# A sliding-window attention stage: new issue orders, probabilities scaled on VectorE, and first loads sorted by use

## The chip, the cores and the metric

The kernel runs on one core of a Trainium2 chip. The metric is the device time of one execution in microseconds (us), lower is better. Four engines compute: TensorE (PE in the profile: matmuls and transposes, results go to PSUM), VectorE (DVE), ScalarE (ACT) and GpSimd (POOL). SyncE (SP) issues most DMAs. Every engine runs its own instruction stream in order, and they wait for one another by semaphores.

## The reference, cut to what matters

Four residual blocks on x of shape (8, 512, 256), float32, one after the other: attention with relative position tables, a mixture of experts, sliding-window attention, the same mixture again. Before each block comes a layernorm. The third block is the one whose instruction orders change:

```
q = rmsnorm(x @ wq.T) * q_gamma ; k = rmsnorm(x @ wk.T) * k_gamma ; v = x @ wv.T      # 16 heads of 64
scores = q @ k.T / 8 + slope[head] * (j - i);  masked unless 0 <= i - j <= 128
attn = softmax(scores);  out = attn @ v;  x = x + out @ wo.T
```

## The kernel before

There are six stages, each with a program per engine: `relative_stage` (tag a), the mixture (`shared_stage` and `expert_stage`, tags fs and fe), `window_stage` (tag b), and the mixture again (gs and ge). Stages don't overlap, except by a few instructions.

`window_stage` works in tiles of 128 queries, 4 to a batch element and 32 in all. With a window of 128, a tile sees its own 128 keys and the 128 before them; the first tile of a batch element has only its own (`lo = 1`). It is called the short tile here, the other three full tiles. For a tile, TensorE does 4 `scores` steps of 4 heads, 8 `probs_T` steps (transposes of the probabilities of 2 heads) and 8 `values` steps. Between them lie the sections of a neighbouring tile: `x` (transposes of the normed input), `q`, `k`, `v` (2 halves each, 6 matmuls of 512 columns a half), `q_T`, `k_T` (2 halves each), `out` (24 matmuls), `xn_T`, and after the last tile of a batch element `gate`. All sections write the one PSUM bank `ps_w`, so each waits until the section before it is copied out (`bank_free`): by VectorE for q, k, q_T, out and gate, by ScalarE for v, k_T and xn_T, by both in turn for x.

The softmax of two heads (index k from 0 to 7) goes: `biased` on VectorE adds the bias and takes the minimum of the negated scores (L1433), `exp` on ScalarE writes `prob` and the row sums (L1315), `inverse` on VectorE takes reciprocals (L1438), `divide` on GpSimd multiplies `prob` of both heads by them (L1377), `probs_T` on TensorE transposes (L1264), VectorE copies that to SBUF (L1442), and `values` multiplies by v (L1275).

What each engine does in which order within a tile is written out in the lists WINDOW_ORDER (TensorE), WINDOW_SCALAR_ORDER, WINDOW_VECTOR_ORDER, WINDOW_POOL_ORDER and WINDOW_SYNC_ORDER. An entry is (step, index, offset in tiles): ("q", 0, 1) is the first half of q for the next tile. `rounds` runs the lists: two partial rounds before the first tile, batch elements 0 and 1 unrolled, 2 to 6 in a hardware loop over the batch element (4 back-edges), 7 unrolled, two rounds behind. In the partial round (-1, 3), the step before the first tile, `first` calls `split_weights`, which casts the weights (ScalarE: high part, VectorE: rest), before that round's own steps.

Besides the divides, GpSimd has the powers (`x_pow`, `pow`, `y_pow`) and `normed`, two instructions of 128x1024 each tile (L1372).

In `relative_stage`, 13 constant tables are loaded after x, all counted by one semaphore `const_in`. TensorE (L1986, then 64 small matmuls L1995 that fold table ends into weights), ScalarE and VectorE wait for all 13. VectorE's set-up (L2376 to L2424) is one long chain, whose last part needs the folded products in `ps_w`; only then does TensorE begin the first q (L2008).

## Time and profile before

| | |
|---|---|
| median of 3 runs | 3860.88 us (3854.68 to 3863.89) |
| the profiled execution's own time | 3863.76 us |
| its span, first to last instruction | 3861.9 us |
| TensorE busy over the span | 3522.0 us (91%) |
| VectorE / ScalarE / GpSimd busy | 2448.2 (63%) / 1814.1 (47%) / 1055.7 (27%) us |
| window stage, 2060 to 3045 us: TensorE / VectorE / ScalarE / GpSimd busy | 915.0 / 623.9 / 482.8 / 363.8 us |

A row of the timeline gives the start and the length in us, the engine, the line, the tiles written and read, the form and the count, and in brackets how long the engine had been idle and what released it. An engine's next instruction can start a little before the listed end of the last, so steps are counted from start to start. PEclk is the share of TensorE's full clock of 2.4 GHz that was granted; 0.5 is 1.2 GHz. Idle time counts only on the engine that everybody waits for.

### The profile page before, as it was taken

The numbers are of one execution on the slowest core, as the hardware profiler recorded it, in microseconds if no ns is written. First come the engines' busy times: TensorE is split into PE (matmuls) and PEld (weight loads), VectorE is DVE, ScalarE is ACT, GpSimd is POOL, SyncE is SP. The second block draws the span as 40 slices with busy tenths as digits, with TensorE's granted clock in tenths as the row PEclk, the third lists the DMA queues.
The fourth block names the chain that finished last, engine by engine and source line by source line (L and its number), as shares of the span: only waits on it lengthen the run. The fifth ranks groups of instructions, "written<-read, shape, count | busy, mean of one in ns | idle before, by whom it ended". The sixth has DMA issues, their size and how long they took to land. (4 is left out here: it accounts for less than half of the span.)

```text
span 3861.9 us, 92551 instructions
## 1 busy us (share of the span) xinstructions
PE 3522.0 (91%) x33008; PEld 2702.7 (70%) x33008; DVE 2448.2 (63%) x5451; ACT 1814.1 (47%) x3734; POOL 1055.7 (27%) x1031
## 2 busy tenths in 40 slices
PE   5999999999997968999995999999999795999998
PEld 3666666666665857888884777667767684888887
DVE  3676666666665666666753666666666576676664
ACT  1665665665663323444442555445545332444443
POOL 0222222222221002333421433334333101243332
PEclk9999999999998989999996999999999897999999
DMA  4565565565564223434422000000000123343441
GB/s 149 162 172 165 155 176 163 159 177 167 155 176 123 89 93 112 131 102 116 120 65 79 16 21 21 19 19 21 21 19 16 60 87 112 110 120 110 118 117 31
DMA packets 349199, 390.10 MB, mean 101 GB/s; under 512 B 155377, under 2 KB 292721, under 8 KB 335345
## 3 DMA queue, kind: packets, MB, share of 16 engines
q1 hardware_dynamic: 324210, 351.18, 29.3%
q0 software_dynamic: 24576, 33.57, 5.0%
q8 instruction: 240, 3.93, 0.4%
q14 instruction: 173, 1.42, 0.1%
HBM read 246.97 MB, written 137.69 MB: 100 GB/s over the span
## 5 line engine op out<-in xcount | busy, mean ns | idle before, releaser
L2278 POOL TENSOR_TENSOR a_below<-a_probT,a_upper 128x512 f32<-128x512 f32 x128 | 164.2, 1283 | 743.8 <-DVE a_probT L2476 553.4
L2213 ACT ACTIVATE a_prob<-a_ps_s,a_low 128x512 f32<-128x512 f32 x512 | 318.3, 692 | 53.1 <-DVE a_low L2496 52.7
L1377 POOL TENSOR_TENSOR b_prob<-b_prob,b_rinv 128x512 f32<-128x512 f32 (+1 forms) x256 | 237.8, 934 | 383.1 <-DVE b_rinv L1438 383.0
L2060 PE MATMUL a_ps_p<-a_ident,a_prob 128*128 128x128 f32 x2048 | 315.8, 288 | 12.9 <-ACT a_band L2190 9.0
L2496 DVE TENSOR_REDUCE a_low<-a_ps_s 128x2 f32<-128x1024 f32 x256 | 313.5, 1225 | 8.8
L1315 ACT ACTIVATE b_prob<-b_score,b_low 128x256 f32<-128x256 f32 (+1 forms) x512 | 241.8, 474 | 125.4 <-DVE b_low L1433 114.4
L2060 PEld LDWEIGHTS a_ps_p<-a_ident,a_prob 128*128 128x128 f32 x2048 | 222.1, 143 | 101.2 <-issue 75.8
L2186 ACT COPY a_probT<-a_ps_p 128x512 f32<-128x512 f32 x352 | 195.1, 590 | 171.6 <-PE a_ps_p L2060 171.0
L1433 DVE CUSTOM_DVE_ANT_0 b_score<-b_ps_s,b_bias 128x256 f32<-128x256 f32 (+1 forms) x512 | 178.1, 386 | 74.3 <-PE b_ps_s L1256 72.1
L2495 DVE TENSOR_TENSOR a_ps_s<-a_ps_s,a_win 128x320 f32<-128x320 f32 (+1 forms) x256 | 135.0, 527 | 133.5 <-PE a_ps_s L2093 131.0
L611 POOL DMA_INDIRECT out<-ge_eo,ge_index_scatter x64 | 120.7, 1886 | 361.4 <-DVE ge_eo L806 346.7
L611 POOL DMA_INDIRECT x<-fe_eo,fe_index_scatter x64 | 120.6, 1884 | 361.6 <-DVE fe_eo L806 347.0
L198 ACT ACTIVATE fe_gelu<-fe_ps_g 128x512 f32<-128x512 f32 x128 | 76.5, 598 | 287.6 <-PE fe_ps_u L177 287.6
L198 ACT ACTIVATE ge_gelu<-ge_ps_g 128x512 f32<-128x512 f32 x128 | 76.5, 598 | 287.5 <-PE ge_ps_u L177 287.5
L1442 DVE COPY b_probT<-b_ps_p 128x512 f32<-128x512 f32 (+1 forms) x256 | 155.5, 617 | 60.8 <-PE b_ps_p L1264 59.3
L214 DVE TENSOR_TENSOR fe_raw<-fe_gelu,fe_ps_u 128x512 f32<-128x512 f32 x128 | 88.0, 687 | 158.0 <-ACT fe_gelu L198 147.0
L214 DVE TENSOR_TENSOR ge_raw<-ge_gelu,ge_ps_u 128x512 f32<-128x512 f32 x128 | 88.0, 687 | 157.8 <-ACT ge_gelu L198 146.8
L1275 PE MATMUL b_ps_o<-b_probT,b_v 128*64 128x128 f32 x1792 | 149.5, 287 | 4.7 <-DVE b_probT L1442 3.8
L187 PE MATMUL fe_ps_d<-fe_d_rest,fe_h_high 128*128 128x256 f32 x512 | 144.3, 282 | 9.8 <-DVE fe_eo L806 6.9
L187 PE MATMUL ge_ps_d<-ge_d_rest,ge_h_high 128*128 128x256 f32 x512 | 144.3, 282 | 9.8 <-DVE ge_eo L806 6.9
L1264 PE MATMUL b_ps_p<-b_ident,b_prob 128*128 128x128 f32 x896 | 147.1, 281 | 4.4 <-POOL b_prob L1377 4.4
L2476 DVE COPY a_probT<-a_ps_p 128x512 f32<-128x512 f32 x160 | 110.4, 691 | 63.2 <-PE a_ps_p L2060 61.4
(437 smaller groups left out, 10433.6 us busy)
## 6 DMA issues: line engine op xcount, KB each, us to landing
a_win<-band SPq DMA_DIRECT2D x128, 384.0 KB, 5.3
prob<-a_prob SPq DMA_DIRECT2D x128, 384.0 KB, 3.7
shift<-a_gbias SPq DMA_DIRECT2D x64, 256.0 KB, 2.0
a_shifted<-shift SPq DMA_DIRECT2D x256, 64.0 KB, 2.1
a_bins<-prob SPq DMA_DIRECT2D x128, 128.0 KB, 3.7
fe_gT<-in_WgT SPq DMA_DIRECT2D x16, 1024.0 KB
fe_uT<-in_WuT SPq DMA_DIRECT2D x16, 1024.0 KB
fe_dT<-in_WdT SPq DMA_DIRECT2D x16, 1024.0 KB, 4.9
```

The costliest lines, as they stand in the source:

```text
L187: last = nc.tensor.matmul(ps_d[t // 2][:, t % 2, :], h[b][:, slot, t * P:(t + 1) * P], d[a][:, j, :], start=(j == 0 and t % 2 == 0 and (a, ...
L214: nc.vector.tensor_tensor(raw[:, slot % 2, :], gelu[:, slot % 2, :], ps_u[slot % 2][:, :], ALU.mult).then_inc(h_ready, 1)
L611: nc.gpsimd.indirect_dma_start(rows_y, bass.IndirectOffsetOnAxis(index[1][:, q, t:t + 1], 0), eo[:, q, t, :], None, bounds_check=B * T - 1 ...
L1315: nc.scalar.activation(prob[:, h % 8, lo * P:], score[:, h % 8, lo * P:], ACT.Exp, bias=low[:, h % 8:h % 8 + 1], scale=-1.0, accum_out=rsu ...
L1377: nc.gpsimd.tensor_tensor(part, part, by_row, ALU.mult).then_inc(divided, 1)
L1433: nc.vector.tensor_tensor_reduce(out=score[:, h % 8, lo * P:], in0=ps_s[k // 2 % 2][r][:, k % 2, lo * P:], in1=bias[:, h, lo * P:], scale= ...
L1442: nc.vector.tensor_copy(probT[:, k % 2, :, lo:, :], ps_p[k % 2][:, :, lo:, :]).then_inc(copied, 1)
L2060: last = nc.tensor.transpose(bank[:, c * P:(c + 1) * P], prob[:, t % 2, h, 32 + c * P:32 + (c + 1) * P], ident[:, :])
L2186: last = nc.scalar.copy(probT[:, t % 2, h, :], ps_p[i][:, :])
L2213: nc.scalar.activation(prob[:, t % 2, h, 32:32 + T], ps_s[pair][:, r, :], ACT.Exp, bias=low[:, h:h + 1]).then_inc(exped, 1)
L2278: nc.gpsimd.tensor_tensor(below[:, t % 2, :, :], probT[:, t % 2, :, t * P:(t + 1) * P], upper[:, :].unsqueeze(1).to_broadcast([P, HG, P]), ...
L2496: nc.vector.reduce_max(low[:, 2 * pair:2 * pair + 2], both[:, :, :], AX.X, negate=True).then_inc(maxed, 1)
```

## The change

Three things are changed together:

1. All five order lists of the window stage are written anew. On TensorE, `v` 1 moves from the tile's end to its middle, `gate` stands directly behind `q_T` 0, and `k_T` 1 ends the tile. On VectorE, `probs_T` 6 and 7 are done at the end of their own tile and no longer at the start of the next; `x_normed` stands first. The load of x is issued two tiles ahead, not three.
2. `divide` moves from GpSimd to VectorE and takes in `inverse`: a reciprocal, a wait for it, and then one `tensor_scalar` for each of the two heads (128x256, in a short tile 128x128) in place of one broadcast `tensor_tensor` over both.
3. Set-up. In `relative_stage` the loads are split over three semaphores: first ident, table, rows, base (`const_in`), then seven small ones (`small_in`), then the two weights (`w_in`); TensorE and VectorE wait for each only where it is used, ScalarE for none. In `window_stage`, ScalarE's `split_weights` and VectorE's `set_gains` now come before all rounds. The first tile's `x_normed` is an entry of round (-1, 3), and so comes behind VectorE's `split_weights`; before it was an entry of the round ahead of that.

```diff
 WINDOW_ORDER = [
     ("scores", 0, 0), ("x", 0, 1), ("scores", 1, 0), ("out", 0, -1), ("probs_T", 0, 0), ("q", 0, 1), ("scores", 2, 0), ("q", 1, 1),
-    ("probs_T", 1, 0), ("values", 0, 0), ("k", 0, 1), ("scores", 3, 0), ("k", 1, 1), ("probs_T", 2, 0), ("values", 1, 0), ("xn_T", 0, -1),
-    ("probs_T", 3, 0), ("v", 0, 1), ("values", 2, 0), ("gate", 0, -1), ("probs_T", 4, 0), ("q_T", 0, 1), ("values", 3, 0), ("probs_T", 5, 0),
-    ("q_T", 1, 1), ("probs_T", 6, 0), ("values", 4, 0), ("k_T", 0, 1), ("values", 5, 0), ("probs_T", 7, 0), ("k_T", 1, 1), ("values", 6, 0),
-    ("values", 7, 0), ("v", 1, 1),
+    ("scores", 3, 0), ("k", 0, 1), ("values", 0, 0), ("probs_T", 1, 0), ("k", 1, 1), ("probs_T", 2, 0), ("values", 1, 0), ("v", 0, 1),
+    ("probs_T", 3, 0), ("values", 2, 0), ("xn_T", 0, -1), ("values", 3, 0), ("v", 1, 1), ("probs_T", 4, 0), ("probs_T", 5, 0), ("q_T", 0, 1),
+    ("gate", 0, -1), ("probs_T", 6, 0), ("values", 4, 0), ("q_T", 1, 1), ("values", 5, 0), ("probs_T", 7, 0), ("k_T", 0, 1), ("values", 6, 0),
+    ("values", 7, 0), ("k_T", 1, 1),
 ]
 WINDOW_SCALAR_ORDER = [
-    ("exp", 0, 0), ("exp", 1, 0), ("exp", 2, 0), ("exp", 3, 0), ("exp", 4, 0), ("q", 0, 1), ("q", 1, 1), ("k", 0, 1), ("exp", 5, 0), ("k", 1, 1),
-    ("xn_T", 0, -1), ("exp", 6, 0), ("v", 0, 1), ("exp", 7, 0), ("high", 0, 0), ("gate_exp", 0, -1), ("k_T", 0, 1), ("k_T", 1, 1), ("high", 1, 0),
-    ("v", 1, 1), ("x", 0, 2),
+    ("exp", 0, 0), ("exp", 1, 0), ("exp", 2, 0), ("exp", 3, 0), ("gate_exp", 0, -2), ("q", 0, 1), ("exp", 4, 0), ("q", 1, 1), ("k", 0, 1),
+    ("k", 1, 1), ("exp", 5, 0), ("v", 0, 1), ("xn_T", 0, -1), ("exp", 6, 0), ("high", 0, 0), ("v", 1, 1), ("exp", 7, 0), ("k_T", 0, 1),
+    ("high", 1, 0), ("k_T", 1, 1), ("x", 0, 2),
 ]
 WINDOW_VECTOR_ORDER = [
-    ("probs_T", 6, -1), ("probs_T", 7, -1), ("rest", 1, -1), ("biased", 0, 0), ("x", 0, 1), ("biased", 1, 0), ("inverse", 0, 0), ("biased", 2, 0),
...
+    ("x_normed", 0, 1), ("rest", 1, -1), ("biased", 0, 0), ("x", 0, 1), ("biased", 1, 0), ("biased", 2, 0), ("divide", 0, 0), ("biased", 3, 0),
+    ("out", 0, -1), ("divide", 1, 0), ("y_stats", 0, -1), ("q", 0, 1), ("divide", 2, 0), ("y_mean", 0, -1), ("biased", 4, 0), ("q", 1, 1),
+    ("probs_T", 0, 0), ("divide", 3, 0), ("x_stats", 0, 2), ("k", 0, 1), ("biased", 5, 0), ("probs_T", 1, 0), ("y_var", 0, -1), ("biased", 6, 0),
+    ("k", 1, 1), ("x_mean", 0, 2), ("gate_end", 0, -2), ("probs_T", 2, 0), ("y_normed", 0, -1), ("mean", 0, 1), ("biased", 7, 0),
+    ("probs_T", 3, 0), ("x_var", 0, 2), ("divide", 4, 0), ("divide", 5, 0), ("divide", 6, 0), ("probs_T", 4, 0), ("rest", 0, 0), ("q_T", 0, 1),
+    ("probs_T", 5, 0), ("gate", 0, -1), ("divide", 7, 0), ("q_T", 1, 1), ("probs_T", 6, 0), ("probs_T", 7, 0),
 ]
 WINDOW_POOL_ORDER = [
-    ("divide", 0, 0), ("divide", 1, 0), ("divide", 2, 0), ("x_pow", 0, 2), ("y_pow", 0, -1), ("divide", 3, 0), ("divide", 4, 0), ("pow", 0, 1),
-    ("normed", 0, 1), ("divide", 5, 0), ("divide", 6, 0), ("normed", 1, 1), ("divide", 7, 0),
+    ("y_pow", 0, -1), ("pow", 0, 1), ("normed", 0, 1), ("x_pow", 0, 2), ("normed", 1, 1),
 ]
 WINDOW_SYNC_ORDER = [
-    ("store", 0, -1), ("store_turned", 0, -2), ("store_normed", 0, -1), ("load", 0, 3),
+    ("store_normed", 0, -2), ("load", 0, 2), ("store", 0, -1), ("store_turned", 0, -1),
 ]
...
+                    elif kind == "divide":
+                        dve.wait_ge(exped, 16 * w + 2 * k + 2)
+                        nc.vector.reciprocal(rinv[:, p, 2 * k:2 * k + 2], rsum[:, p, 2 * k:2 * k + 2]).then_inc(rinv_ready, 1)
+                        dve.wait_ge(rinv_ready, 8 * w + k + 1)
+                        for r in range(2):
+                            h = 2 * k + r
+                            part = prob[:, h % 8, lo * P:]
+                            scaled = nc.vector.tensor_scalar(part, part, rinv[:, p, h:h + 1], None, ALU.mult)
+                        scaled.then_inc(divided, 1)
...
-                    set_gains()
                     split_weights()
                 unit(b, t)
 
+            set_gains()
             rounds(nc.vector, first)
...
+        first_loads = ((ident, const["ident"]), (whole_table, table_d), (rows, rows_d), (whole_base, base_d))
+        small_loads = ((upper, const["upper"]), (iota, const["iota"]), (number, const["token"]), (scale, const["row_scale"]),
+                       (bins_w, bins_d), (bins_b, bins_base_d), (vbase, vbase_d))
+        w_loads = ((wT, wT_d[0]), (wv, wT_d[1]))
```

## Rows read from the trace of the kernel before

**Rows 1.** Busy time of each engine by stretch: one query tile each, PEclk the granted clock
```profile
2220.41:2249.10 28.69, 26.03 (x178) 18.59 (x177) 16.02 (x69) 13.41 (x49) 8.81 (x13) 1.00 0.06 20
2249.10:2277.43 28.33, 28.23 (x210) 20.93 (x209) 20.46 (x70) 15.18 (x48) 12.21 (x13) 1.00 0.06 19
2421.38:2453.60 32.22, 28.74 (x210) 20.96 (x209) 19.97 (x67) 15.81 (x49) 12.22 (x13) 1.00 0.06 19
2453.60:2484.91 31.31, 28.76 (x177) 21.00 (x177) 16.41 (x69) 13.02 (x48) 8.85 (x13) 0.89 0.06 19
```

**Rows 2.** Timeline in a short tile: start, length, engine, line
```profile
2227.84 0.69 DVE L1414 COPY b_raw<-b_ps_w 128x512 f32<-128x512 f32 x1 [0.30 <-PE b_ps_w L1191]
...
2228.59 0.50 PE L1191 MATMUL b_ps_w<-b_wq_high,b_x_rest 128*128 128x512 f32 x1
```

**Rows 3.** Timeline near the end of a full tile
```profile
2272.44 1.28 DVE L1442 COPY b_probT<-b_ps_p 128x512 f32<-128x512 f32 x2
...
2273.79 0.66 PE L1264 MATMUL b_ps_p<-b_ident,b_prob 128*128 128x128 f32 x4
...
2274.28 0.60 PE L1198 MATMUL b_ps_w<-b_ident,b_normed 128*128 128x128 f32 x4
...
2274.81 1.09 PE L1275 MATMUL b_ps_o<-b_probT,b_v 128*64 128x128 f32 x16
```

**Rows 4.** Timeline of the first stage's start
```profile
16.13 0.17 DVE L2376 MEMSET a_v<- 128x128 f32 x1 [0.17 <-DVE a_prob L2374]
...
21.24 2.40 DVE L2380 TENSOR_TENSOR a_win<-a_probT,a_win 128x1040 f32<-128x1040 f32 x2 [4.95 <-DMA a_scale<-in_row_scale]
...
23.02 13.65 PE L1995 MATMUL a_ps_w<-a_probT,a_k_up 128*128 128x4 f32 x64
...
35.05 0.24 DVE L2415 TENSOR_SCALAR a_query_same<-a_iota,a_residue 128x32 f32<-128x32 f32 x1
36.71 0.51 DVE L2420 COPY a_k_low<-a_ps_w 128x32 f32<-128x32 f32 x4 [1.43 <-PE a_ps_w L1995]
...
41.14 0.79 PE L2008 MATMUL a_ps_w<-a_x_high,a_w_rest 128*128 128x512 f32 x1 [4.47 <-DVEq L2431]
```

**Rows 5.** DMA issues of the first 60 us: count, KB, us from issue to landing
```profile
a_win<-in_a_base SPq DMA_DIRECT2D x1, 1040.0 KB, 11.5
```

**Rows 6.** Timeline of the window stage's start
```profile
2074.25 2.18 ACT L1342 CAST b_wo_high<-b_prob 128x512 fp32r<-128x512 f32 x4 [0.24 <-DMA b_prob<-in_b_woT]
...
2078.49 0.77 PE L1191 MATMUL b_ps_w<-b_wq_high,b_x_rest 128*128 128x512 f32 x1 [11.12 <-DVE b_x_rest L161]
```

**Rows 7.** Groups of instructions by line and form, GpSimd and VectorE: busy us, mean ns
```profile
L1372 POOL TENSOR_SCALAR b_normed<-b_raw,b_rrms 128x1024 f32<-128x1024 f32 x64 | 71.6, 1119 | 15.3 <-POOL b_rrms L1366 14.1 <-DVE b_rinv L1438 1.2
...
L1363 POOL TENSOR_TENSOR b_rstd<-b_var,b_minus_half 128x1 f32<-128x1 f32 x32 | 17.5, 548 | 31.3 <-DVE b_var L1399 31.3
...
L1438 DVE RECIPROCAL b_rinv<-b_rsum 128x2 f32<-128x2 f32 x256 | 37.7, 155 | 12.1 <-ACT b_prob L1315 11.0 <-issue 0.9
...
L2340 DVE TENSOR_SCALAR a_xi<-a_xi,a_in_mv,a_in_rstd 128x256 f32<-128x256 f32 x32 | 11.3, 415 | 1.4 <-POOL a_in_rstd L2297 1.4
...
L842 DVE TENSOR_SCALAR fe_eo<-f_st,f_thr 128x512 f32<-128x512 f32 x1 | 0.5, 487 | 0.0
...
L2415 DVE TENSOR_SCALAR a_query_same<-a_iota,a_residue 128x32 f32<-128x32 f32 x1 | 0.2, 236 | 0.0
```

**Rows 8.** Timeline: VectorE and GpSimd at the same time
```profile
2204.17 1.04 POOL L1377 TENSOR_TENSOR b_prob<-b_prob,b_rinv 128x512 f32<-128x512 f32 x1 [0.22 <-DVE b_rinv L1438]
...
2204.58 0.78 DVE L1403 TENSOR_SCALAR b_xn<-b_x,b_mv,b_rstd 128x256 f32<-128x256 f32 x1
```

**Rows 9.** Timelines of VectorE and TensorE around a loop back-edge
```profile
2447.75 1.29 DVE L1442 COPY b_probT<-b_ps_p 128x512 f32<-128x512 f32 x2 [2.08 <-PE b_ps_p L1264]
...
2448.49 1.26 PE L1275 MATMUL b_ps_o<-b_probT,b_v 128*64 128x128 f32 x16 [1.06 <-DVE b_probT L1442]
...
2453.60 0.71 PE L1256 MATMUL b_ps_s<-b_kT,b_qT 64*128 64x128 f32 x8 [2.27 <-issue]
```

More of the change, by code:

```diff
@@ L912 @@
+    ("high", 1, 0), ("k_T", 1, 1), ("x", 0, 2),
 ]
 WINDOW_VECTOR_ORDER = [
-    ("probs_T", 6, -1), ("probs_T", 7, -1), ("rest", 1, -1), ("biased", 0, 0), ("x", 0, 1), ("biased", 1, 0), ("inverse", 0, 0), ("biased", 2, 0),
-    ("gate_end", 0, -2), ("biased", 3, 0), ("inverse", 1, 0), ("out", 0, -1), ("y_stats", 0, -1), ("probs_T", 0, 0), ("x_stats", 0, 2),
-    ("inverse", 2, 0), ("x_mean", 0, 2), ("q", 0, 1), ("y_mean", 0, -1), ("x_var", 0, 2), ("biased", 4, 0), ("q", 1, 1), ("y_var", 0, -1),
@@ L917 @@
-    ("probs_T", 1, 0), ("inverse", 3, 0), ("biased", 5, 0), ("x_normed", 0, 2), ("inverse", 4, 0), ("k", 0, 1), ("y_normed", 0, -1), ("k", 1, 1),
-    ("probs_T", 2, 0), ("biased", 6, 0), ("mean", 0, 1), ("probs_T", 3, 0), ("biased", 7, 0), ("inverse", 5, 0), ("gate", 0, -1),
-    ("inverse", 6, 0), ("probs_T", 4, 0), ("q_T", 0, 1), ("inverse", 7, 0), ("rest", 0, 0), ("q_T", 1, 1), ("probs_T", 5, 0),
+    ("x_normed", 0, 1), ("rest", 1, -1), ("biased", 0, 0), ("x", 0, 1), ("biased", 1, 0), ("biased", 2, 0), ("divide", 0, 0), ("biased", 3, 0),
@@ L1342, in split_weights @@
                     nc.scalar.copy(wo[0][:, i:i + 2, :].rearrange("p k c -> p (k c)"), flat[:, i * C:(i + 2) * C]).then_inc(wo_high, 1)
-            def first(b, t):
-                if isinstance(b, int) and (b, t) == (-1, NT - 1):
-                    split_weights()
-                unit(b, t)
-            rounds(nc.scalar, first)
+            split_weights()
+            rounds(nc.scalar, unit)
         @block.gpsimd
@@ L1372, in unit @@
                         nc.gpsimd.tensor_scalar(normed[:, k, :], raw[:, k, :], rrms[:, k:k + 1], 1.0, ALU.mult, ALU.mult).then_inc(normed_ready, 1)
-                    elif kind == "divide":
-                        reach_alone(pool, rinv_ready, 8 * w + k + 1)
-                        part = prob[:, 2 * (k % 4):2 * (k % 4) + 2, lo * P:]
-                        by_row = rinv[:, p, 2 * k:2 * k + 2].unsqueeze(2).to_broadcast([P, 2, (2 - lo) * P])
-                        nc.gpsimd.tensor_tensor(part, part, by_row, ALU.mult).then_inc(divided, 1)
                     elif kind == "y_pow":
@@ L1769, in relative_stage @@
         o_taken = s.sem("o_taken")
-        loads = ((ident, const["ident"]), (upper, const["upper"]), (iota, const["iota"]), (number, const["token"]), (wT, wT_d[0]), (wv, wT_d[1]),
-                 (rows, rows_d), (whole_table, table_d), (whole_base, base_d), (bins_w, bins_d), (bins_b, bins_base_d), (vbase, vbase_d),
-                 (scale, const["row_scale"]))
-        assert len(loads) == LOADS
+        first_loads = ((ident, const["ident"]), (whole_table, table_d), (rows, rows_d), (whole_base, base_d))
+        small_loads = ((upper, const["upper"]), (iota, const["iota"]), (number, const["token"]), (scale, const["row_scale"]),
+                       (bins_w, bins_d), (bins_b, bins_base_d), (vbase, vbase_d))
+        w_loads = ((wT, wT_d[0]), (wv, wT_d[1]))
+        assert len(first_loads + small_loads + w_loads) == LOADS
         block = ctx.enter_context(s.programs())
@@ L1824, in _ @@
             sp.dma_start(xi[:, :, :], by_token(x_d, 0)).then_inc(xi_in, 16)
-            for tile, dram in loads:
-                sp.dma_start(tile[tuple(slice(None) for _ in tile.shape)], dram).then_inc(const_in, 16)
+            for loads, sem in ((first_loads, const_in), (small_loads, small_in), (w_loads, w_in)):
+                for tile, dram in loads:
+                    sp.dma_start(tile[tuple(slice(None) for _ in tile.shape)], dram).then_inc(sem, 16)
             for sem in (x1_out, yn_out, ynT_out):
@@ L2151, in _ @@
         def _(act):
-            act.wait_ge(const_in, 16 * len(loads))
             def empty(kind, b, g, k=0):
```

9 lines of the change are left out of this document (7 added, 2 removed).

## Prediction

> **What bounds the kernel now.** I read the page's busy shares first, then the busy time of single query tiles in the window stage, then the timelines of the three places that the change touches: the start of the first stage, the start of the window stage, and its tiles.
>
> TensorE is busy for 91% of the span, but in the window stage that share hides two limits. A full tile takes 28.33 us with TensorE busy for 28.23 of them [rows 1]: TensorE never waits for anybody there, and no order can make the tile shorter (its neighbour took 28.37; I use 28.35). A short tile has fewer matmuls and still takes 28.69 us, with TensorE busy for 26.03 [rows 1]. What holds it is the one bank `ps_w`: after a section its result is copied out, and the next section starts only then. The copy of q starts at 2227.84 and takes 0.69 us, and TensorE's next section starts 0.75 us after the copy began [rows 2]. I added up the short tile section by section: x 1.4 us, out 3.6, six halves of q, k and v at 2.3 to 2.5, four of q_T and k_T at 1.3 to 1.6, xn_T 1.0, gate 2.5, each from its own start to the start of the next, gives 28.5 us, nearly all of the 28.69. So the short tile can't get much shorter either by an order; it only gets longer when a copy comes late.
>
> VectorE does most of these copies in order with everything else. It is busy for 20.46 us of the full tile and 16.02 of the short one [rows 1]: it has room, but not much.
>
> The tiles at a loop back-edge are longer: 32.22 us for the last one of an iteration and 31.31 us for the short one behind it, the latter at a mean granted clock of 0.89 [rows 1]. In the first of them TensorE waits 1.06 us for a copy of probabilities and then 2.27 us for nothing that the profile shows, its own branch [rows 9]. The copy was late since VectorE had its own back-edge just ahead of `probs_T` 6, and began only at 2447.75 after 2.08 us idle [rows 9]. There are 4 such places.
>
> **The change, part by part.** *Start of the first stage.* VectorE's last memset ends at 16.13 + 0.17 = 16.30 us; then it waits for all 13 tables until 21.24 [rows 4]. TensorE waits as long. From there VectorE's chain runs to 35.05 + 0.24 = 35.29, 14.05 us; the folding on TensorE ends at 23.02 + 13.65 = 36.67 [rows 4], 15.43 us after 21.24. VectorE goes on at 36.71 and the first q starts at 41.14 [rows 4]. Now only x, ident, table, rows and base are ahead: 3.6 MB instead of the 5.0 MB that were ahead of and with base when it landed at 5.38 + 11.5 = 16.9 us [rows 5]. In proportion they land at 13 to 14.5. VectorE then starts at 16.30 and is through at 30.35, TensorE at 14.5 + 15.43 = 29.9. So 36.71 becomes 30.4 to 30.6: 6.1 us gained. Bounds: if base still lands at 16.9, TensorE is through at 32.3, and 4.4 are left; if the small loads land no sooner than the last table did, at 21.24, VectorE has about 11.4 us left from there, and 4.1 are left. The two weights come last, 5.9 MB in all as before, so by 21 us, long before 30. Everything behind moves up by the same amount. Value -6.1, bounds -4.1 to -6.3.
>
> *Start of the window stage.* ScalarE's casts no longer wait for the first x_high, but the last four need wo, which landed at 2074.25 [rows 6], and the DMA order is the same. So VectorE ends its rests at most 0.4 us sooner (it was through at 2078.05). But the first tile's `x_normed` now stands behind them, and with it the transposes, ScalarE's cast and VectorE's rest of x: 0.42 + 0.69 + 0.37 + 0.42 and some 0.15 of waits, 2.05 us, where only the rest of 0.42 was left. The first q, at 2078.49 [rows 6], comes 1.3 us later; bounds 0.9 (if VectorE is through earlier still) to 1.7.
>
> *The divide itself.* It leaves GpSimd, where one took 1.04 us [rows 8], off the path but for its latency. On VectorE no such instruction is in the trace at this size, so its price comes from neighbours of the same kind. A `tensor_scalar` with one per-row scalar takes 487 ns for 512 columns and 236 for 32 [rows 7]: 0.52 ns a column, so 353 ns for 256 and 286 for 128. The next instruction starts about 0.08 us before the listed end (two copies of 0.68 end to end take 1.28 [rows 3]), so each costs 0.27 (0.21) us of the queue. With a reciprocal of 155 ns [rows 7] and the wait for it, 0.19, a divide is 0.73 us in a full tile and 0.61 in a short one; `inverse`, 0.08 of queue, goes. The upper bound is the nearest row with 256 columns and two such scalars, 415 ns [rows 7]: 0.33 each, 0.85 a divide. Eight divides add 5.2 us to VectorE's 20.46 less 0.7 for `x_normed` and `y_normed`, which now seldom meet GpSimd: 25 us of 28.3.
>
> By the Trainium skill (VectorE: DVE Perf Modes, section on the TRN2 errata) a float32 SBUF op that runs two elements a cycle costs 58 + 128 cycles at 256 columns, 0.19 us. No row has this; by it a full tile's late stretch below would be 0.6 us shorter, and the stall that I find there gone.
>
> *Full tile.* I laid VectorE's new list against TensorE's with these prices. Up to `probs_T` 3 VectorE catches up several times, so the eight copies and divides there are hidden. The tight stretch is behind it. TensorE's work after `probs_T` 3: six `values` at 0.59 (a pair together 1.03), four transposes of probabilities at 0.49, four of q and k at 0.53 [rows 3], v at 1.6, xn_T at 0.27: 9.4 us, so `probs_T` 3 is done at 28.35 - 9.4 = 18.95 of the tile. VectorE then has eight copies of 0.60 [rows 3], four divides of 0.73 and `x_var`, 7.8 us without a pause, to 26.8; after that TensorE has values 7 and k_T 1, 1.05 us. That fits inside 28.35 with 0.4 to spare.
>
> But GpSimd's `normed` is in the same stretch. It isn't free of VectorE: `x_normed` on VectorE, 415 ns elsewhere [rows 7], took 0.78 us when it started in the middle of a GpSimd instruction, and ended 0.15 us behind that one's end, 2204.17 + 1.04 against 2204.58 + 0.78 [rows 8]. In the new lists `x_pow` waits for `x_var`, just ahead of divides 4 to 6, takes 548 ns, and `normed` of 1119 ns [rows 7] follows at once: it starts about 0.9 us behind `x_var`, in the middle of divide 5. Whoever comes first, one of VectorE's four instructions there ends behind `normed`: 0.9 to 1.0 us later. The copies behind it move with it, 26.8 becomes 27.75, and the tile ends at 27.75 + 0.1 + 1.05 = 28.9: 0.55 us longer. The queue behind holds the copies that TensorE waits for (`q_T`, `probs_T` 5 to 7), so nothing hides it. I take 0.45 for 24 tiles, 10.8 us; bounds 0 (no collision, or spare time enough) to 1.0 (415 ns instead of 353 makes the eight late instructions 0.5 longer).
>
> The Trainium skill (SBUF — State Buffer, "Who interferes with whom") says that a VectorE instruction in a two-port mode and a GpSimd instruction exclude each other for their whole length. The row on `x_normed` agrees; without that rule the 10.8 us would be 0.
>
> *Short tile.* The same sections give the same sum, 28.5; the move of `gate` behind `q_T` 0 changes what fills the waits, not their number. The collision delays the copy of q_T 0 by 0.5, and TensorE waits for it directly: 0.2 longer than now after the 0.3 that better fillers give. 8 tiles, 1.6 us; bounds -2.4 to 5.
>
> *Back-edges.* VectorE's branch now lies behind `probs_T` 7, beside TensorE's own, so the 1.06 us goes, 4 times: -4.2. The 2.27 stays. Less idle time there may spare one or the other fall of the clock: -1, bounds -6 to +4. The exit of the stage has the same chain as before: 0, plus or minus 1.
>
> *Sum.* -6.1 + 1.3 + 10.8 + 1.6 - 4.2 - 1 = +2.4 us. The profiled execution took 3863.76 us itself, so 3866.2 by its measure; it lay 2.9 above the median of 3860.88, so 3863.3, rounded to 3863.
>
> **Rivals.** *A, nothing collides or VectorE has more room than I think:* full tiles stay at 28.35, short ones gain 0.3. -6.1 + 1.3 - 2.4 - 4.2 - 1 = -12.4, 3848. For it: 0.4 us spare in my own count, and the start of `normed` depends on 0.2 us either way. Against: `x_pow` and `normed` are tied to the same `x_var` as the divides.
>
> *B, VectorE becomes the bound:* the price is 415 ns and the collision full. Full tiles +1.0, short ones +0.6: -6.1 + 1.3 + 24 + 4.8 - 4.2 - 1 = +18.8, 3880. It decides from about 26.9 us of VectorE work in a full tile, or 0.4 us of delay behind `probs_T` 3. For it: eight late instructions in a row, each wait uncounted. Against: TensorE's stalls give VectorE time back at the start of the next tile.
>
> *C, the loads don't come sooner:* if DMA works the new order as late as the old one, set-up gains only 2 us or nothing and the rest stands: +6 to +8.5, 3867 to 3869. Against: transfers of the first 20 us are steady, and the order of issue is the order of landing.
>
> **How the numbers follow.** My forecast has 0.45 (own range 3854 to 3872), A 0.20, B 0.23, C 0.07, and 0.05 is left for what I don't see. 3863 is the forecast's. The range goes from A's to B's middle, 3847 to 3882; outside lie about 2 in 10. 0.2% is 7.7 us, what a measurement can just tell from no change. Faster (under 3853.2): A and a little of the forecast's, 0.23. Slower (over 3868.6): B, a fifth of the forecast's, half of C and the rest, 0.36. Same: 0.41.
>
> **What would show it.** In the first stage: VectorE's `tensor_tensor` L2380 near 16.4 us and the first q near 35. In the window stage: first q 1.3 us later against the stage's first load; `tensor_scalar` on prob near 353 ns in the median, but a part of 0.9 or more, those that end 0.15 us behind a `normed`; full tiles of 28.7 to 28.9 us, with TensorE's waits for q_T, k_T's turn and the last probabilities; no wait of 1.06 us ahead of the back-edge. I am wrong if full tiles stay at 28.35 (A), if they pass 29.2 (B), or if the first q of the kernel stays at 41 us (C).

## The result: 0.35% slower

| | before | after |
|---|---|---|
| median of 8 runs each, on the same chip | 3854.05 us (3843.55 to 3863.89) | 3869.89 us (3861.73 to 3874.4) |
| after / before | | 1.0035, 95% interval 1.002 to 1.005 |
| profiled execution, its span | 3863.76, 3861.9 us | 3865.24, 3863.5 us |

By the ratio that is +13.5 us (7.7 to 19.3). The forecast was 3863 with a range of 3847 to 3882: the range held the time, but the likeliest case said "no change that can be told", and it is a small loss. The forecast as a change was +2.4 us, added to a median of before of 3860.88; over eight runs that median is 3854.05, so the two times lie closer together (3863 and 3869.89) than the two changes do (+2.4 and +13.5). The two profiled executions are only 1.6 us apart. The profile of before was taken in an execution 9.7 us above that kernel's median here, that of after in one 4.7 us below its own, so the spans can't be compared, only the stages.

**Starts of the stages after.** The first group is the first stage (the rows to hold against [rows 4]), the second the window stage ([rows 6]).

```profile
14.24 13.65 PE L1998 MATMUL a_ps_w<-a_probT,a_k_up 128*128 128x4 f32 x64
...
16.07 2.37 DVE L2382 TENSOR_TENSOR a_win<-a_probT,a_win 128x1040 f32<-128x1040 f32 x2
...
34.45 0.77 PE L2012 MATMUL a_ps_w<-a_x_high,a_w_rest 128*128 128x512 f32 x1 [6.55 <-DVEq L2435]
```

```profile
2058.77 2.18 ACT L1341 CAST b_wo_high<-b_prob 128x512 fp32r<-128x512 f32 x4 [0.67 <-DMA b_prob<-in_b_woT]
...
2061.83 0.41 DVE L1393 TENSOR_SCALAR b_xn<-b_x,b_mv,b_rstd 128x256 f32<-128x256 f32 x1
...
2063.95 0.76 PE L1190 MATMUL b_ps_w<-b_wq_high,b_x_rest 128*128 128x512 f32 x1 [0.97 <-DVE b_x_rest L161]
```

The first q starts at 34.45 us, 6.7 us sooner. The window stage's first q comes 5.18 us behind the cast of wo; before it was 2078.49 - 2074.25 = 4.24. Measured from the end of TensorE's last product of the mixture ahead, it is 34.68 us against 33.69: 1.0 later.

**Tiles after.** Busy time by stretch, one tile each, columns as in [rows 1]: an unrolled short tile, the full tile behind it, the next one; then, in the loop, the tile that holds the back-edge, the short one behind it, and a second tile of a batch element.

```profile
2202.86:2231.46 28.60, 26.15 (x177) 18.57 (x176) 20.57 (x86) 13.48 (x49) 4.02 (x5) 1.00 0.06 20
2231.46:2260.65 29.19, 28.68 (x209) 20.89 (x209) 25.37 (x86) 15.25 (x49) 4.14 (x5) 1.00 0.06 19
2260.65:2289.28 28.63, 28.49 (x210) 20.89 (x209) 24.40 (x83) 15.22 (x49) 4.17 (x5) 1.00 0.07 20
2405.73:2437.57 31.84, 28.63 (x210) 20.93 (x209) 25.34 (x84) 15.98 (x50) 4.14 (x5) 0.99 0.06 19
2437.57:2471.66 34.09, 31.59 (x176) 23.15 (x177) 20.56 (x85) 12.85 (x47) 4.02 (x5) 0.80 0.06 18
2347.24:2376.84 29.60, 28.82 (x209) 20.93 (x208) 25.52 (x86) 15.29 (x49) 4.14 (x5) 1.00 0.06 20
```

"Second tile" is from here on the one behind the short tile, and a plain full tile is the third or fourth outside the loop. Plain full tiles went from 28.35 to 28.63 us, second tiles from 28.33 to 29.19 (in the loop 28.59 to 29.60). The second tile of the first batch element, for which VectorE has no expert operations (`gate_end`) to do, took only 28.63. The back-edge tiles stayed as long as they were (31.84, 32.24, 31.97 and 31.77 us against 32.22, 31.88, 31.52 and 31.67); the short tile behind the first of them runs at a mean granted clock of 0.80 where it was 0.89. I added the tiles up by kind from the second tile of the stage to its end: second tiles +7.0 us, third +2.4, fourth +1.4, short +7.5, and 2.2 in the last tile and what follows it; 912.4 us became 932.9. Ahead of that, from the first q to the second tile, after took 53.0 us where before took 56.9: there TensorE ran 25.1 us at 1.2 GHz, not 35.8.

**The collision.** VectorE and GpSimd in the late stretch of a full tile of after:

```profile
2280.29 0.62 DVE L1436 TENSOR_SCALAR b_prob<-b_prob,b_rinv 128x256 f32<-128x256 f32 x2
...
2281.01 1.41 DVE L1436 TENSOR_SCALAR b_prob<-b_prob,b_rinv 128x256 f32<-128x256 f32 x2
2281.03 1.24 POOL L1367 TENSOR_SCALAR b_normed<-b_raw,b_rrms 128x1024 f32<-128x1024 f32 x1
...
2282.52 0.62 DVE L1436 TENSOR_SCALAR b_prob<-b_prob,b_rinv 128x256 f32<-128x256 f32 x2
```

Two divisions take 0.62 us together, but 1.41 when `normed` starts beside them. They end at 2282.42, 0.15 us behind the end of `normed` at 2282.27, as `x_normed` did in [rows 8]. By the Trainium skill (SBUF — State Buffer, "Who interferes with whom") a VectorE instruction in a two-port mode and a GpSimd instruction exclude each other for a whole instruction; the trace agrees.

A plain full tile has one such long collision. A second tile has two: the division ahead of that one meets the other half of `normed`, here in a second tile.

```profile
2250.76 1.12 POOL L1367 TENSOR_SCALAR b_normed<-b_raw,b_rrms 128x1024 f32<-128x1024 f32 x1 [0.40 <-POOL b_rrms L1361]
...
2251.11 1.18 DVE L1436 TENSOR_SCALAR b_prob<-b_prob,b_rinv 128x256 f32<-128x256 f32 x2
...
2252.39 1.40 DVE L1436 TENSOR_SCALAR b_prob<-b_prob,b_rinv 128x256 f32<-128x256 f32 x2
```

**TensorE's waits**, 2100 to 2960 us, of after, then of before (in total, how often, the longest):

```profile
PE b_ps_s L1255 <- issue: 12.0, 4, 3.3
PE b_ps_w L1219 <- DVE b_qT L1409: 7.1, 7, 1.0
...
PE b_ps_p L1263 <- DVE b_probT L1441: 4.0, 16, 0.3
PE b_ps_p L1263 <- DVE b_prob L1436: 2.1, 6, 0.5
```

```profile
PE b_ps_s L1256 <- issue: 8.1, 4, 2.3
...
PE b_ps_o L1275 <- DVE b_probT L1442: 3.6, 4, 1.1
...
PE b_ps_w L1220 <- ACT b_v L1304: 2.1, 7, 0.3
```

The copy ahead of the branch (3.6 us in 4 waits) is no longer waited for, but the branch itself costs TensorE 3.0 us each in place of 2.0. The expert section (L1219) now waits for the copy of q_T 0, 7.1 us in all, where it waited 2.1 for ScalarE's v.

### The profile page after: what moved, and what is told of

Its sections match the earlier page's. It is cut to its first block and busy times, and to the rows that moved or that the text cites. A ratio compares the mean times of both kernels' runs of the same rounds, so it can differ in the third digit from the quotient of the medians.

```text
span 3863.5 us, 92396 instructions
## 1 busy us (share of the span) xinstructions
PE 3521.3 (91%) x33008; PEld 2698.4 (70%) x33008; DVE 2597.0 (67%) x5963; ACT 1816.7 (47%) x3734; POOL 821.3 (21%) x775
## 3 DMA queue, kind: packets, MB, share of 16 engines
q1 hardware_dynamic: 324210, 351.18, 29.3%
## 5 line engine op out<-in xcount | busy, mean ns | idle before, releaser
L1436 DVE TENSOR_SCALAR b_prob<-b_prob,b_rinv 128x256 f32<-128x256 f32 (+1 forms) x512 | 185.1, 404 | 9.1
L1300 ACT ACTIVATE b_square<-b_raw 128x512 f32<-128x512 f32 x128 | 80.9, 632 | 223.1 <-DVE b_raw L1404 223.1
L1371 POOL TENSOR_TENSOR b_y_rstd<-b_y_var,b_minus_half 128x1 f32<-128x1 f32 x32 | 17.6, 549 | 733.4 <-DVE b_y_var L1457 733.4
L1263 PE MATMUL b_ps_p<-b_ident,b_prob 128*128 128x128 f32 x896 | 144.1, 281 | 11.2 <-DVE b_probT L1441 5.1
```

The source lines that it names most:

```text
L1436: scaled = nc.vector.tensor_scalar(part, part, rinv[:, p, h:h + 1], None, ALU.mult)
```

## The experiments

Medians are given with the ratio to the kernel before, from runs on the same chip.

**1. The three parts apart.** `setup_only` has the loads and the set-up of after, and all five lists and the division as before.

> Only the set-up part of the change, order lists and divide as in the kernel before. If the loads split over three semaphores carry the gain by the work they free (the first q came 6.7 us sooner in the changed kernel), this kernel is 6 to 8 us faster than before (ratio 0.998). If the higher granted clock that the changed kernel showed behind its first q (15.0 us ahead by the first scores instead of 6.7) belongs to the earlier start as well, 14 to 16 us (ratio 0.996). If set-up gives nothing beyond what executions differ by, ratio 1.000.

`pool_divide` has after's lists, but the division is GpSimd's:

```diff
 WINDOW_VECTOR_ORDER:  every ("divide", k, 0) -> ("inverse", k, 0)
 WINDOW_POOL_ORDER = [
-    ("y_pow", 0, -1), ("pow", 0, 1), ("normed", 0, 1), ("x_pow", 0, 2), ("normed", 1, 1),
+    ("divide", 0, 0), ("divide", 1, 0), ("divide", 2, 0), ("divide", 3, 0), ("y_pow", 0, -1), ("pow", 0, 1), ("normed", 0, 1),
+    ("x_pow", 0, 2), ("divide", 4, 0), ("divide", 5, 0), ("divide", 6, 0), ("normed", 1, 1), ("divide", 7, 0),
```

> The changed kernel with the divides back on GpSimd and a reciprocal in their place on VectorE; all other lists and the set-up stay. Theory of the prediction (VectorE's divides and their collision with normed cost about 0.3 to 0.5 us in each full tile): unrolled full tiles fall from 28.63 to 28.35 us, in-loop ones from 28.9 to 28.6, and the kernel is 8 to 12 us faster than the changed one (ratio to before 0.999 to 1.001). Rival (the new lists lose the time: gate behind q_T 0, gate_end late, branches together): tiles keep 28.6 and 29.6 us, ratio to before 1.003 as with the change.

`old_lists_vector` is the kernel before, with VectorE's division in the places of its `inverse` and none on GpSimd.

> The kernel before with one edit: VectorE multiplies by the inverse sums where its list had the reciprocal; all lists (less the divides on GpSimd) and set-up as before. If the divide alone costs what VectorE lacks in room, full tiles take 28.6 to 29 us and the kernel is 6 to 20 us slower than before (ratio 1.0015 to 1.005). If the lists are what costs, tiles stay at 28.35 and the ratio at 1.000.

| | median | ratio | plain full tile | second tile in the loop |
|---|---|---|---|---|
| setup_only | 3845.05 | 0.9971 (0.996 to 0.9983) | 28.36 | 28.60 |
| pool_divide | 3869.9 | 1.0045 (1.0029 to 1.0062) | 28.84 | 30.07 |
| old_lists_vector | 3932.87 | 1.021 (1.019 to 1.023) | 31.38 | 32.51 |

The set-up alone is a gain of 11.2 us (6.6 to 15.4), and `setup_only` beats both kernels. The gain lies between the 6 to 8 us and the 14 to 16 us of its two theories and decides neither. So lists and division together cost some 24.7 us. `pool_divide` was to be 8 to 12 us faster than after by the prediction's theory and is no faster; its rival, that the new lists lose the time, had the time right, and the tiles are longer than even the rival said. `old_lists_vector` lost some 80 us where 6 to 20 were expected. Neither half does well without the other: VectorE's division in the old places makes q's and q_T's copies late (TensorE's waits for `b_raw`, the copied-out q and k, 25.5 us, for `b_qT` 25.2), and GpSimd's division in the new lists comes late itself (`b_ps_p <- POOL b_prob`: 14.3 us in 43 waits).

**2. The collision or the load?** `short_normed` lets `normed` cover 64 of its 1024 columns from the third tile on, which takes the collision away and leaves VectorE's list alone. The other columns of q and k stay unscaled.

> The changed kernel, but from the third tile on GpSimd's two normed instructions cover 64 of 1024 columns each, so q and k are mostly stale there: work left out. Theory: the collision of normed with the divides costs 0.3 us and more in each tile; the one instruction of about 1.15 us that each tile has among its divides goes back to 0.35, full tiles to 28.35, in all 8 to 12 us less than the changed kernel (ratio to before 0.999 to 1.001). Rival (the delay is absorbed, the cost is VectorE's work itself or the lists): tiles keep 28.6 us and the kernel is within 2 us of the changed one.

`short_divide` leaves `normed` whole and shortens the divisions; it leaves most of the probabilities undivided. In a plain full tile its short divisions no longer meet `normed` either (the longest take 0.26 us in those shown below), so it takes away load and collision together:

```diff
-                            part = prob[:, h % 8, lo * P:]
+                            part = prob[:, h % 8, lo * P:lo * P + 8]
```

> The kernel after, with each of VectorE's products by an inverse sum taken over 8 columns of a head's 256 (128 in first tiles) in both stages' window part, so that the rest of the probabilities stays undivided; the instruction count is as in the kernel after. Theory D (VectorE's load by the division, some 4.5 us a tile more than before, makes the loss): full tiles fall to 28.35 and the second tiles too, run about 3850, ratio 0.998 to 0.999. Theory N (the new TensorE order alone costs 0.2 us a full tile, and the clock's drops in the short tile are its too): full tiles stay at 28.55, the short tiles behind the branch over 33, run 3860 to 3866, ratio 1.0015 to 1.003.

`short_normed`: 3866.33, ratio 1.0026 (1.0016 to 1.0036). Full tiles 28.57 us, second tiles in the loop 28.71 instead of 29.60. `short_divide`: 3853.0, ratio 0.999 (0.9974 to 1.0005). So the 8 to 12 us that `short_normed` was to save did not come (by the ratios it saved 3.5), and `short_divide` came out as its theory D had it, but for the short tiles. The tiles of `short_divide` in the order of those above (short, second, third, with the back-edge, short behind it):

```profile
2209.12:2238.78 29.66, 27.25 (x177) 19.52 (x176) 19.70 (x86) 13.47 (x49) 4.00 (x5) 0.94 0.06 19
2238.78:2267.10 28.32, 28.25 (x210) 20.89 (x209) 23.36 (x86) 15.14 (x49) 4.00 (x5) 1.00 0.06 19
2267.10:2295.46 28.36, 28.28 (x210) 20.92 (x209) 21.87 (x83) 15.10 (x49) 4.00 (x5) 1.00 0.07 20
2410.73:2442.32 31.59, 28.36 (x210) 20.90 (x209) 22.90 (x84) 15.88 (x50) 4.00 (x5) 0.99 0.06 19
2442.32:2476.15 33.83, 31.38 (x176) 23.03 (x177) 19.77 (x85) 12.84 (x47) 3.99 (x5) 0.80 0.06 18
```

Full tiles are back at 28.34, second ones too (28.45 in the loop). So TensorE's new order costs a full tile nothing, and what it lost is VectorE's time for the division: 2.5 us of busy time in the third tile. Without the collision alone, 0.23 of the 0.29 us stay in a plain full tile. Where it may go is seen in VectorE's group of probability copies over the first three full tiles, after and then `short_divide`:

```profile
L1441 DVE COPY b_probT<-b_ps_p 128x512 f32<-128x512 f32 x24 | 16.1, 680 | 1.0 <-PE b_ps_p L1263 1.0
```

```profile
L1441 DVE COPY b_probT<-b_ps_p 128x512 f32<-128x512 f32 x24 | 16.1, 681 | 3.0 <-PE b_ps_p L1263 3.0
```

The copies have two thirds of the idle time ahead of them gone (3.0 us became 1.0; the kernel before has 6.0). That TensorE loses its 0.29 us by waiting for them is argued, not shown: the waits view has none in a plain full tile, where TensorE is busy for 28.49 of 28.63 us. Second tiles are another matter: there TensorE waits 0.3 us each for a copy of probabilities and, in the loop, for a division, and either remedy takes most of the loss (29.60 to 28.71 and to 28.45). The short tiles stay long in both kernels, so neither collision nor load explains them.

**3. Two places in the lists.** `gate_end_early` moves the three last expert operations on VectorE out of the second tile's middle:

```diff
 WINDOW_SCALAR_ORDER:  ("gate_exp", 0, -2) behind exp 3   ->  ("gate_exp", 0, -1) behind k_T 0
 WINDOW_VECTOR_ORDER:  ("gate_end", 0, -2) ahead of probs_T 2  ->  ahead of biased 3
```

> The kernel after, with the three last VectorE operations of the expert scores (sum, reciprocal, product) moved forward in the second tile of a sequence, from behind the third copy group to the start of the tile, and the exponential that they wait for moved from that tile to the end of the first one. Theory G (in second tiles the +1.0 us over the kernel before comes of these three operations standing in VectorE's busiest stretch, ahead of a copy that TensorE waits for): second tiles fall from 29.2 (29.6 in the loop) to about 28.6, 8 of them, so the run takes 4 to 7 us less than the kernel after, 3863 to 3866, ratio to the kernel before 1.0015 to 1.0025. Theory H (the loss is the collision with the normalization's products alone, or TensorE's list): second tiles stay at 29.2 and more, run 3868 to 3871.

`gate_first` moves the expert section ahead of q_T:

```diff
-    ... ("probs_T", 4, 0), ("probs_T", 5, 0), ("q_T", 0, 1), ("gate", 0, -1), ("probs_T", 6, 0), ...
+    ... ("probs_T", 4, 0), ("gate", 0, -1), ("probs_T", 5, 0), ("q_T", 0, 1), ("probs_T", 6, 0), ...
 WINDOW_VECTOR_ORDER:  ("gate", 0, -1) from behind probs_T 5 to ahead of probs_T 4
```

> The kernel after, with TensorE's expert-logit section moved ahead of the turning of the queries (behind the fifth pair's transposes), and VectorE's maximum and subtraction with it. Theory Q (TensorE stands at the expert section because the PSUM buffer that it fills is emptied by the copy of the turned queries, up to 1.0 us in the short tile, and the pause is what drops the clock there): the 7.1 us of waits at the expert section's first matmul go, the half-clock episodes about 27 us behind each branch go too, the short tiles behind the branch fall from 32.9 to 34.2 to about 31, and the run takes 5 to 9 us less than the kernel after. Theory R (the clock drop comes of the expert section itself or of the branch, wherever the section stands): the low episodes stay, the short tile keeps over 33 us, and the wait moves to the next section; within 2 us of the kernel after.

`gate_end_early`: 3870.33, 1.0041 (1.0023 to 1.0058). Second tiles fell only from 29.60 to 29.25 in the loop and from 29.19 to 28.82 outside. Theory G holds for 0.36 of the 1.0 us (7 tiles, under 3 us, and the run doesn't show it). The trace says more than the time: the earlier of the two long collisions is gone, its two divisions take 0.62 us again outside the loop where they took 1.18, and in its place TensorE waits for the copy of `out`, which now stands behind the moved operations (4.4 us in 13 waits, 2.1 in 7 in after). So those operations cost second tiles a second collision, and 0.36 us is the least they cost. `gate_first`: 3867.34, 1.0029 (1.0013 to 1.0045). The section waits 3.2 us instead of 7.1 (for ScalarE's v), and the short tiles behind the branch take 32.05, 32.15, 32.38 and 33.48 us where after had 34.09, 32.88, 30.18 and 34.20: mean 32.5 against 32.8. The half-clock stretches, in which the granted clock was 1.2 GHz, stay, in most cases shorter (3.4 us, not 6.8). That is theory R, nearly.

**4. The branch.** `early_copies` is `setup_only` with one move on VectorE:

```diff
 WINDOW_VECTOR_ORDER = [
-    ("probs_T", 6, -1), ("probs_T", 7, -1), ("rest", 1, -1), ...
+    ("rest", 1, -1), ...
-    ... ("q_T", 1, 1), ("probs_T", 5, 0),
+    ... ("q_T", 1, 1), ("probs_T", 5, 0), ("probs_T", 6, 0), ("probs_T", 7, 0),
```

> The kernel before with the new set-up of the first stage (all lists and the division on GpSimd as before), and only VectorE's last two copies of turned probabilities moved from the head of the next tile to the end of their own, ahead of the branch. Theory P (the prediction's: TensorE's 1.06 us at values 6 behind each branch is the copy that VectorE makes late, and 4 of them come back): 4 us less than with the set-up alone, which was 3845, so 3841, ratio to the kernel before 0.996. Theory O (TensorE is late at the branch by itself, its instruction fetch takes 2.3 us and more there, so the freed wait turns into its own issue time, as in the kernel after, where the branch tile stayed at 31.8 to 32.2): the branch tile stays at 31.7 to 32.2, full tiles stay at 28.35, time within 1.5 us of the set-up alone.

3846.73, 0.9981 (0.9967 to 0.9996). The back-edge tile fell to 30.90, 30.89, 30.92 and 30.70 us (`setup_only`: 31.3 to 31.8), so 0.7 of the 1.06 comes back where the rest of the list is old; the short tile behind it took 30.8 to 32.9 (30.9 to 31.2), so it is lost again there, and the run shows no gain: theory O had the time right, and theory P a part of the tile. TensorE at the branch, first after, then `early_copies`:

```profile
2434.07 0.65 PE L1197 MATMUL b_ps_w<-b_ident,b_normed 128*128 128x128 f32 x4
2437.57 1.22 PE L1255 MATMUL b_ps_s<-b_kT,b_qT 64*128 64x128 f32 x8 [2.84 <-issue]
```

```profile
2431.19 0.40 PE L1191 MATMUL b_ps_w<-b_wv_rest,b_x_high 128*128 128x512 f32 x1
2433.84 1.23 PE L1256 MATMUL b_ps_s<-b_kT,b_qT 64*128 64x128 f32 x8 [2.25 <-issue]
```

The idle time is 2.84 us behind four transposes and 2.25 behind twelve 512-column products, of which the row shows the last. `v_last` puts those products back to the end of after's tile:

```diff
-    ... ("values", 3, 0), ("v", 1, 1), ("probs_T", 4, 0), ...  ("values", 6, 0), ("values", 7, 0), ("k_T", 1, 1),
+    ... ("values", 3, 0), ("probs_T", 4, 0), ...  ("values", 6, 0), ("k_T", 1, 1), ("values", 7, 0), ("v", 1, 1),
 WINDOW_SCALAR_ORDER:  ("v", 1, 1) behind k_T 1
```

> The kernel after, with the second half of the values' projection (twelve 512-column products) moved from TensorE's middle to the end of the tile, behind the last keys' transposes, as in the kernel before, and ScalarE's copy of it with it. Theory T (TensorE's sequencer runs ahead of the array only by the work that stands queued: with four transposes at the end it has 2.8 us of empty time at the branch, with twelve long products 2.0 to 2.3): the branch tile falls from 31.8 to 32.2 to about 31.2 and its four issue waits from 12.0 us to under 9; total 2 to 3 us less than the kernel after if nothing is lost where the products stood. Rival U (they filled TensorE's time there while VectorE divides and copies, so that its waits for the fifth to seventh pairs grow): full tiles go from 28.63 to 28.8 and more, and the run is 3 to 8 us slower than the kernel after.

3981.95, 1.0323 (1.0295 to 1.035). A full tile of it, and TensorE's waits from 2100 to 2960 us:

```profile
2156.07:2187.71 31.64, 29.09 (x210) 20.87 (x209) 24.40 (x83) 15.13 (x48) 4.17 (x5) 1.00 0.06 18
```

```profile
PE b_ps_p L1263 <- DVE b_prob L1436: 34.5, 47, 1.0
PE b_ps_w L1190 <- ACT b_kT L1306: 29.3, 25, 1.2
PE b_ps_s L1255 <- issue: 9.7, 4, 2.5
```

Both theories were right in kind. The branch costs 2.4 us instead of 3.0, and a plain full tile 3.0 us more, 112 us in all where rival U had said 3 to 8. In the middle of the tile `v` 1 is what TensorE does while VectorE divides (34.5 us of waits for divisions), and at the end it stands one step behind `k_T` 1 and waits for ScalarE's copy of that out of `ps_w` (29.3 us).

**5. No branch at all.** The window stage's loop written out, for both sets of lists:

```diff
-            with engine.Fori(2, B - 1) as b:
-                for t in range(NT):
-                    unit(b, t)
-            for t in range(NT):
-                unit(B - 1, t)
+            for b in range(2, B):
+                for t in range(NT):
+                    unit(b, t)
```

> The kernel before with the new set-up alone, and the window stage's loop over sequences written out, so that no engine branches in it. Theory B (a branch costs the 3.2 us by which its tile is longer, and another 2.3 us in the short tile behind it, by the clock that falls after the pause; and waits on register values cost 0.2 us a tile in the loop): branch tiles fall to 28.35, short tiles to 28.7 to 30, tiles of the loop from 28.58 to 28.35, together 18 to 26 us, run 3820 to 3828, ratio to the kernel before 0.991 to 0.993. Rival F (the written-out code has to be fetched, the fetches disturb loads and stores or TensorE's queue): single tiles of 30 us and more remain, run 3835 and more.

> The kernel after with the window stage's loop over sequences written out. Theory B (half of the loss in the loop is the clock behind the branch, in the branch tile's missing gain and in short tiles of 33 and 34 us): short tiles go to 28.6 to 29.9, second tiles from 29.6 to 29.2, full tiles from 28.88 to 28.63, run 3838 to 3848, and the distance to the set-up with the old lists written out shrinks from 25 to 13 to 18 us. Rival E (the drops of the clock in the short tile come of the expert section alone): short tiles stay at 32 and more in most sequences though no branch is there, and the distance stays at 20 us and more.

`setup_unrolled`: 3823.48, 0.9917 (0.9897 to 0.9936). `after_unrolled`: 3842.14, 0.9968 (0.9954 to 0.9981). They are 0.54% and 0.67% below their looped kernels, 21 and 26 us, times within theory B's ranges in both. Two tiles of `setup_unrolled` (fourth, short), and two of `after_unrolled`:

```profile
2748.23:2776.61 28.38, 28.28 (x209) 20.96 (x208) 19.86 (x67) 15.09 (x48) 12.23 (x13) 1.00 0.06 19
2776.61:2806.30 29.69, 27.35 (x178) 19.47 (x177) 16.19 (x69) 13.41 (x49) 8.84 (x13) 0.94 0.06 19
```

```profile
2529.72:2558.34 28.62, 28.48 (x209) 20.89 (x208) 24.39 (x83) 15.21 (x49) 4.17 (x5) 1.00 0.06 20
2558.34:2588.04 29.70, 27.38 (x177) 19.57 (x177) 20.82 (x85) 13.44 (x49) 4.02 (x5) 0.94 0.06 19
```

The distance between the two sets of lists is 18.7 us without the branch, and was 24.7 with it. That a part of the loss hung on the branch isn't shown: by the two intervals the 24.7 has some 7 us of uncertainty either way, and in the profiled executions the window stage, from the end of the mixture on, differs by 19.8 us with the branch and by 21.0 without. Without it six of seven short tiles of after's lists still have a half-clock stretch at the expert section, three of seven with the old lists: 208.8 against 203.7 us for the seven. In the looped `setup_only`, with the old lists, all seven have one. The last run has both edits, `after_unrolled` and `gate_first`.

> The kernel after with both edits: the loop written out, and the expert section ahead of the turning of the queries. With the loop written out but the old place of that section, short tiles were 29.7 to 29.8 us (one 31.3), each with one 3.4 us stretch at half clock at the expert section, and TensorE waited there 6.7 us in 7 places. Theory W (that wait of 1.0 us is what lets the clock fall in a short tile): the wait shrinks to 0.5, most of the half-clock stretches go, short tiles fall to 28.6 (as two of the three unrolled ones did in the looped kernel with this edit), 5 to 9 us less than with the loop written out alone, run 3833 to 3837. Theory X (the clock falls at the expert section by its own small matmuls and the copies around it, and the longer wait changes nothing): short tiles stay at 29.7, a 3.4 us stretch in each, run 3841 to 3843.

3840.67, 0.9953 (0.9935 to 0.9972). The wait halved (3.2 us); seven short tiles took 28.6, 29.7, 29.4, 30.6, 28.6, 30.5 and 28.6 us, 206.1 together. Three have no slow stretch now, two have one of 6.8 us. That is some 3 us less in the profile, and the time doesn't show it against `after_unrolled`. Theory W's 5 to 9 us did not come, and theory X's stretch in each tile didn't either. Single executions scatter more than that: `pool_divide`, `short_normed` and `short_divide` all have the expert section behind `q_T` 0 and wait 0.8 us there, and their seven short tiles took 212.4, 223.8 and 221.2 us. So whether the wait has a share in the falls of the clock stays open.

## Why the forecast was nearly right, and what in it was not

The closeness of 3863 to 3869.89 is in part luck. The set-up gave 11.2 us where 6.1 were counted, and lists and division cost 24.7 where 1.3 + 10.8 + 1.6 - 4.2 - 1 = 8.5 were; the two misses partly offset one another, and the median of before that the sum was added to was 6.8 us above that of eight runs. As a change, +13.5 us lies nearer to rival B's +18.8 than to the forecast's +2.4.

Step by step, the predicted term and what the runs gave. Where no run is named, the measured number is after less before in the two profiled executions, one of each, and those of the window stage add up to +17.6:

| step | predicted | measured |
|---|---|---|
| first stage | -6.1 | first q -6.7; the whole set-up -11.2 (6.6 to 15.4) by `setup_only` |
| start of the window stage | +1.3 | first q +1.0 |
| from the first q to the second tile | 0 | -3.9 |
| full tiles | +10.8 | +10.3, in 19 tiles, without the back-edge tiles and the last |
| short tiles | +1.6 | +7.5 |
| back-edges | -4.2 | +0.5 |
| clock | -1 | inside the other rows |
| exit of the stage | 0, plus or minus 1 | +2.2 |

How much of the -3.9 and the +2.2 is the lists' can't be told: over the profiled executions the first of these stretches took 51.7 to 56.9 us with the old lists and 51.6 to 56.0 with the new ones (`v_last` 59.4), the last tile and what follows it 30.7 to 34.1 and 31.8 to 34.5.

*First stage.* VectorE's chain started at 16.07 us where I had 16.3, and q at 34.45. The transposes began at 12.48, sooner than my 13 to 14.5. The -6.1 lies just outside the interval of `setup_only`, so the set-up gave more than this step, and the profile doesn't say where. In the window stage the first q of `setup_only` comes 33.20 us behind the mixture, 0.5 sooner than before. As for the first stage, its end is at 1245.7 us before and at 1237.1 in `setup_only`, but at 1233.0 in `old_lists_vector`, which has the old set-up, and between 1228.8 and 1240.8 in the others. One execution's scatter there is as large as the gain.

*Full tiles.* The sum is right, its reasons only in part, and that it is so close is luck: plain tiles lost less than the 0.45 us taken, second tiles twice as much. The price was right: 353 ns in the median for 256 columns and 286 for 128, both as predicted. These groups are of after's window stage, all forms apart:

```profile
L1436 DVE TENSOR_SCALAR b_prob<-b_prob,b_rinv 128x256 f32<-128x256 f32 x384 | 143.4, 415 | 6.8
...
L1436 DVE TENSOR_SCALAR b_prob<-b_prob,b_rinv 128x128 f32<-128x128 f32 x128 | 41.8, 369 | 2.3
```

Their means hold the collisions, once or more a tile. One of them happened where I had put it; the second one in second tiles I had not seen. But the collision isn't what a plain full tile pays for (0.06 of its 0.29 us, `short_normed`); the division's own time is (`short_divide`). I had written that eight copies and divisions ahead of `probs_T` 3 are hidden and 0.4 us are to spare behind it. There was less to spare than that. The 24 tiles aren't alike either: 12 of them lost 0.3 and the seven second tiles behind the first batch element 0.9 to 1.0 (the rest are the four back-edge tiles and the last). Those seven alone have `gate_end` in VectorE's list, which I never costed (0.36 at least by `gate_end_early`), and two long collisions where the others have one. In the aside that reckons with 0.19 us an instruction the sum is off too: eight instructions, each 0.16 us shorter, make 1.3 us, not 0.6.

*Short tiles.* This step failed: "changes what fills the waits, not their number". I did see that TensorE would wait directly for the copy of q_T 0, but priced it at 0.2 a tile. It is 1.0 instead of the 0.3 us at that section before, and behind it TensorE's clock fell to 1.2 GHz in four of seven short tiles: transposes of q and k that took 0.60 us ([rows 3]) take 1.12 there. TensorE in the short tile behind the first back-edge of after is shown below. How much of the +7.5 is the lists' and how much is this execution's stays open: the same seven tiles took 211.6 us before and 213.4 in `setup_only`, but 217.3 in `early_copies`, where TensorE's list is the old one, and 212.4 in `pool_divide`, where it is the new one.

```profile
2461.49 0.66 PE L1197 MATMUL b_ps_w<-b_ident,b_normed 128*128 128x128 f32 x4
2463.18 2.37 PE L1219 MATMUL b_ps_w<-b_gwT,b_ynT 128*128 128x16 f32 x16 [1.03 <-DVE b_qT L1409]
...
2466.62 1.12 PE L1197 MATMUL b_ps_w<-b_ident,b_normed 128*128 128x128 f32 x4
```

*Back-edges.* "The 2.27 stays" was wrong. The wait of 1.06 us went, as forecast, but TensorE's idle time at the branch grew from 2.0 to 3.0 us, since the new list ends with four short transposes and the old one with twelve long products; `v_last` gives 2.4 with the products back. What TensorE does in that idle time no run shows. Behind the longer pause the clock fell for 6.8 us and not 3.4 in two of four places.

*Rivals.* A: `short_divide` shows what it needed, full tiles at 28.35, and even that kernel is only 4 us below the one before, not 12, and its interval holds 1: its short tiles took 221.2 us and the branch gives nothing back. B, VectorE as the bound, holds for second tiles only. C fell with the first row of the profile.

## What to carry on

Change one thing of such a bundle at a time on the chip: here the new set-up was worth 11 us alone and lists with division took 25 back. The best version found is neither kernel, but the old lists, the new set-up, and the loop over sequences written out: 3823.5 us, 0.8% below the kernel before. When a step moves to the engine that makes the copies, look not at its busy share (24.4 of 28.6 us seemed to leave room) but at the idle time ahead of each copy that TensorE waits for, in every kind of tile by itself. And what stands last on TensorE before a branch matters: long work hides part of it, short work less.
